# A gated cross-attention layer with a mixture of experts: expert weights loaded by another engine, in another order, and router steps moved between softmax sums

## The reference

```python
x = x + tanh(g_xattn[0]) * attn(ctx_768, layernorm(x), mask, ...)
xf = layernorm(x).reshape(-1, 256)
probs = softmax(xf @ w_router); topk_w, topk_idx = top_k(probs, 2)
h = gelu(einsum('te,ieh->tih', xf, w1) + b1)      # 8 experts
out = sum_over_experts((einsum('tih,ihe->tie', h, w2) + b2) * weights)
x = x + tanh(g_ffn[0]) * out
```

## Time and profile before

| | |
|---|---|
| median of 3 runs | 947.58 us (947.28 to 949.43) |
| the profiled execution | 946.13 us |
| its span | 944.6 us, TensorE's mean clock 0.975 |
| TensorE busy | 863.5 us (91%) |
| VectorE busy | 647.5 us (69%) |
| ScalarE busy | 514.6 us (54%) |
| GpSimd busy | 354.5 us (38%) |
| DMA | 70.3 MB, mean 74 GB/s |

### The profile page before, as it was taken

How to read it: one execution, slowest core, us unless ns; L and a number is a source line. 1 busy time by engine, 2 the same in 40 slices (tenths; PEclk the granted TensorE clock), 3 DMA queues, 4 the chain that set the end, 5 groups by cost and what they waited for, 6 DMA issues and landing times.

```text
span 944.6 us, 19200 instructions
## 1 busy us (share of the span) xinstructions
PE 863.5 (91%) x5968; PEld 662.2 (70%) x5968; DVE 647.5 (69%) x1500; ACT 514.6 (54%) x1371; POOL 354.5 (38%) x270
## 2 busy tenths in 40 slices
PE   3898899998999998999899998999999999999865
PEld 3654445554455444544369998999999999999855
DVE  6767766767867668665886787765757675765655
ACT  2668675787757877477652843433434343433432
POOL 2333223332375234652073247342422442242433
PEclk8899999999999999999999998999999999999977
DMA  4801000130012201120053368352432553252441
GB/s 123 237 1 48 1 1 1 45 92 1 12 51 74 90 23 35 57 79 1 1 182 67 80 175 230 62 139 45 124 55 45 133 128 55 45 139 45 123 114 20
DMA packets 58793, 70.30 MB, mean 74 GB/s; under 512 B 11536, under 2 KB 51856, under 8 KB 58736
## 3 DMA queue, kind: packets, MB, share of 16 engines
q0 software_dynamic: 17520, 32.49, 15.5%
q1 hardware_dynamic: 40224, 37.10, 13.7%
q10 hardware_dynamic: 992, 0.00, 0.1%
HBM read 44.04 MB, written 26.31 MB: 74 GB/s over the span
## 4 chain that ended last, share of the span: by engine, by line
PE 51%; issue 15%; DVE 12%; POOL 10%; ACT 5%; DMA 4%; DVEq 1%; POOLq 0%; SPq 0%; ACTq 0%
PE psS L1642 19%; PE psF L1838 9%; PE psO L1838 9%; POOL rr L635 6%; PE psO L1775 4%; PE psS L1759 4%; POOL routed L645 3%; DVE p_sum L1115 3%; PE psF L1642 2%; DMA b_raw<-in_L_ffn_b 2%; DMA lnf<-routed 2%; PE psF L1806 1%; ACT sq L807 1%; ACT p_ring L851 1%; DMA xr<-in_x 1%
## 5 line engine op out<-in xcount | busy, mean ns | idle before, releaser
L868 ACT ACTIVATE V<-psS,b_col 128x256 f32<-128x256 f32 x280 | 117.2, 471 | 222.8 <-PE psS L1642 209.3
L659 POOL DMA_INDIRECT out<-V,token_i x70 | 121.0, 1729 | 260.7 <-DVE V L1304 247.7
L635 POOL TENSOR_TENSOR rr<-ssm,minus_half 128x4 f32<-128x4 f32 (+1 forms) x72 | 119.9, 1666 | 255.5 <-DVE ssm L1079 255.4
L851 ACT ACTIVATE p_ring<-psS,shift 128x1024 f32<-128x1024 f32 x128 | 136.7, 1112 | 75.9 <-PE psS L1759 72.7
L1775 PE MATMUL psO<-p_ring,V 128*64 128x512 f32 x576 | 150.3, 619 | 4.6 <-ACT o_sb L839 4.6
L1115 DVE TENSOR_TENSOR p_sum<-p_sum,p_ring 128x1024 f32<-128x1024 f32 (+1 forms) x112 | 136.0, 1214 | 0.7
L1838 PE MATMUL psF<-ln_hi,K 128*128 128x256 f32 x560 | 123.0, 283 | 0.0
L1759 PE MATMUL psS<-Q,K 64*128 64x512 f32 x864 | 121.7, 413 | 0.1
L1759 PEld LDWEIGHTS psS<-Q,K 64*128 64x128 f32 x864 | 77.0, 187 | 61.8 <-issue 43.5
L1838 PE MATMUL psO<-ln_hi,K 128*128 128x256 f32 x560 | 120.0, 278 | 0.0
L1642 PE MATMUL psS<-w_hi 128*128 128x256 f32 x280 | 83.2, 297 | 20.1 <-DVE w_lo L1267 13.4
(11 more groups left out here) (294 smaller groups left out, 1804.3 us busy)
## 6 DMA issues: line engine op xcount, KB each, us to landing
lnf<-routed SPq DMA_DIRECT2D x35, 258.0 KB, 2.8
xr<-in_L_ffn_w POOLq DMA_DIRECT2D x7, 1024.0 KB, 7.2
xn<-in_L_ffn_w POOLq DMA_DIRECT2D x7, 1024.0 KB, 8.8
routed<-pad_rows SPq DMA_DIRECT2D x17, 258.0 KB, 8.6
xr<-in_x SPq DMA_DIRECT2D x8, 512.0 KB, 4.6
xb<-in_x SPq DMA_DIRECT2D x4, 1024.0 KB, 6.0
out<-xb SPq DMA_DIRECT2D x4, 1024.0 KB, 4.7
xr<-in_L_ffn_w SPq DMA_DIRECT2D x4, 1024.0 KB, 6.7
```

The source lines that it names most:

```text
L635: pool.tensor_tensor(rr[0:p, c % 2, n], ssm[0:p, c % 2, n], minus_half[0:p, n], ALU.pow).then_inc(rr_ready, 1)
L659: pool.indirect_dma_start(out_rows, bass.IndirectOffsetOnAxis(ap=token_i[:, m:m + 1], axis=0), y_out[:, m, :], None, bounds_check=NTOK - 1 ...
L851: act.activation(p_ring[0:p, u % RING, :], psS[u % 2][0:p].rearrange("p a n -> p (a n)"), ACT.Exp, bias=bias).then_inc(exp_done, 1)
L868: act.activation(g32[:, q % 2, (c % 2) * TM:(c % 2 + 1) * TM], psH[q][:, (c % 2) * TM:(c % 2 + 1) * TM], ACT.Gelu_apprx_tanh, bias=b1_col[ ...
```

## The change

1. SyncE issues the weight loads of all experts; GpSimd none. One count per buffer (`w1_loaded`, `w2_loaded`, `b1_loaded`) takes the place of one for four loads. Each engine waits for the part that it reads.
2. w1 is loaded once w1 is cut, w2 and b2 once w2 is cut (and b2 copied), apart from each other.
3. In SyncE's list these loads stand between loads of rows; in its loop tile t first loads the next w1 (if t is an expert's last tile), then rows of tile t+2, then w2, b2, b1.
4. On VectorE, in the last window, `add_probabilities` of a group goes ahead of its router steps, `router_rows` to its group's end, and the two cuts of w2 from groups 3 and 4 to 5 and 8.

The diff:

```diff
@@ -546,11 +548,30 @@
 
-    def load_weights(e):
+    def load_w1(e):
         sp.wait_ge(w1_ready, (e - 1) * 2 * KEPT + 2)
+        sp.dma_start(w1_raw, w1[e].rearrange("(c p) h -> p c h", p=P)).then_inc(w1_loaded, 16)
+
+    def load_w2(e):
         sp.wait_ge(w2_ready, (e - 1) * 2 * KEPT + 2)
         sp.wait_ge(w_cut, e)
+        sp.dma_start(w2_raw, w2[e].rearrange("(c p) d -> p c d", p=P)).then_inc(w2_loaded, 16)
+        sp.dma_start(b2_raw[:], b2[e:e + 1].to_broadcast([P, D])).then_inc(w2_loaded, 16)
+
+    def load_b1(e):
         sp.wait_ge(b1_taken, e)
-        sp.dma_start(w1_raw, w1[e].rearrange("(c p) h -> p c h", p=P)).then_inc(raw_loaded, 16)
-        sp.dma_start(w2_raw, w2[e].rearrange("(c p) d -> p c d", p=P)).then_inc(raw_loaded, 16)
-        sp.dma_start(b1_raw[:], b1[e].rearrange("(c p) -> p c", p=P)).then_inc(raw_loaded, 16)
-        sp.dma_start(b2_raw[:], b2[e:e + 1].to_broadcast([P, D])).then_inc(raw_loaded, 16)
+        sp.dma_start(b1_raw[:], b1[e].rearrange("(c p) -> p c", p=P)).then_inc(b1_loaded, 16)
+
+    def next_w1(t, turn, e):
+        sp.wait_ge(w1_ready, t * 2 + 4)
+        sp.sem_inc(passed, 1)
+        sp.dma_start(w1_raw, w1[bass.ds(e, 1)].rearrange("a (c p) h -> p (a c) h", p=P)).then_inc(w1_loaded, 16)
+
+    def next_w2(t, turn, e):
+        sp.wait_ge(w2_ready, t * 2 + 4)
+        sp.sem_inc(passed, 1)
+        sp.wait_ge(w_cut, turn + (KE + 1))
+        sp.wait_ge(b1_taken, turn + (KE + 1))
+        sp.sem_inc(passed, 1)
+        sp.dma_start(w2_raw, w2[bass.ds(e, 1)].rearrange("a (c p) d -> p (a c) d", p=P)).then_inc(w2_loaded, 16)
+        sp.dma_start(b2_raw[:], b2[bass.ds(e, 1)].to_broadcast([P, D])).then_inc(w2_loaded, 16)
+        sp.dma_start(b1_raw[:], b1[bass.ds(e, 1)].rearrange("a (c p) -> p (a c)", p=P)).then_inc(b1_loaded, 16)
 
@@ -564,3 +585,5 @@
     load_rows(1, kept_row(1))
-    load_weights(1)
+    load_w1(1)
+    load_w2(1)
+    load_b1(1)
     sp.wait_ge(scattered, (B - 1) * (32 * T))
@@ -570,5 +593,8 @@
     load_rows(4, kept_row(4))
+    load_w1(2)
+    load_w2(2)
     load_rows(5, kept_row(5))
-    load_weights(2)
+    load_b1(2)
     load_rows(6, kept_row(6))
+    load_w1(3)
     sp.wait_ge(pads_known, 1)
@@ -576,3 +602,5 @@
         pad(e)
+    load_w2(3)
     load_rows(7, kept_row(7))
+    load_b1(3)
     for e in range(NE // 2, NE):
@@ -580,3 +608,2 @@
     load_rows(8, kept_row(8))
-    load_weights(3)
     sp.wait_ge(scattered, B * (32 * T))
@@ -585,5 +612,21 @@
     load_rows(KTILES, sp.value_load(tile_row[0:1, KTILES:KTILES + 1], min_val=0, max_val=NE * REGION - TM))
+    load_w1(KE + 1)
+    load_rows(KTILES + 1, sp.value_load(tile_row[0:1, KTILES + 1:KTILES + 2], min_val=0, max_val=NE * REGION - TM))
+    load_w2(KE + 1)
+    load_b1(KE + 1)
     tiles = sp.value_load(tile_count[0:1, 0:1], min_val=SURE, max_val=NTILES)
-    with sp.Fori(KTILES, NTILES - 1) as t, sp.If(t + 1 < tiles):
-        load_rows(t + 1, sp.value_load(tile_row[0:1, bass.ds(t + 1, 1)], min_val=0, max_val=NE * REGION - TM))
+    with sp.Fori(KTILES, NTILES) as t, sp.If(t < tiles):
+        turn = sp.value_load(tile_switch[0:1, bass.ds(t, 1)], min_val=0, max_val=NE - 1)
+        after = sp.value_load(tile_next[0:1, bass.ds(t, 1)], min_val=0, max_val=NE - 1)
+        with sp.If(turn > 0):
+            with sp.If(turn < NE - 1):
+                next_w1(t, turn, after)
+            sp.sem_inc(passed, 1)
+        with sp.If(t + 2 < tiles):
+            load_rows(t + 2, sp.value_load(tile_row[0:1, bass.ds(t + 2, 1)], min_val=0, max_val=NE * REGION - TM))
+        with sp.If(turn > 0):
+            with sp.If(turn < NE - 1):
+                next_w2(t, turn, after)
+            sp.sem_inc(passed, 1)
+        sp.sem_inc(passed, 1)
     sp.wait_ge(x_loaded, tiles * 16)
@@ -648,8 +691,2 @@
 
-    def load_expert(e):
-        pool.dma_start(w1_raw, w1[bass.ds(e, 1)].rearrange("a (c p) h -> p (a c) h", p=P)).then_inc(expert_loaded, 16)
-        pool.dma_start(w2_raw, w2[bass.ds(e, 1)].rearrange("a (c p) d -> p (a c) d", p=P)).then_inc(expert_loaded, 16)
-        pool.dma_start(b1_raw[:], b1[bass.ds(e, 1)].rearrange("a (c p) -> p (a c)", p=P)).then_inc(expert_loaded, 16)
-        pool.dma_start(b2_raw[:], b2[bass.ds(e, 1)].to_broadcast([P, D])).then_inc(expert_loaded, 16)
-
     def add_rows(t):
@@ -661,16 +698,2 @@
 
-    def add_and_load(t):
-        turn = next_expert(pool, t)
-        add_rows(t)
-        with pool.If(turn > 0):
-            with pool.If(turn < NE - 1):
-                pool.wait_ge(w1_ready, t * 2 + 4)
-                pool.sem_inc(passed, 1)
-                pool.wait_ge(w2_ready, t * 2 + 4)
-                pool.sem_inc(passed, 1)
-                pool.wait_ge(w_cut, turn + (KE + 1))
-                pool.wait_ge(b1_taken, turn + (KE + 1))
-                pool.sem_inc(passed, 1)
-                load_expert(pool.value_load(tile_next[0:1, bass.ds(t, 1)], min_val=0, max_val=NE - 1))
-
     first_root(0)
@@ -712,12 +735,7 @@
     pool.wait_ge(x2_stored, 16 * B)
-    pool.wait_ge(w1_ready, 2 * KTILES + 2)
-    pool.wait_ge(w2_ready, 2 * KTILES + 2)
-    pool.wait_ge(w_cut, KE + 1)
-    pool.wait_ge(b1_taken, KE + 1)
-    load_expert(KE + 1)
     with pool.Fori(KTILES, SURE) as t:
-        add_and_load(t)
+        add_rows(t)
     tiles = count_of(pool)
     with pool.Fori(SURE, NTILES) as t, pool.If(t < tiles):
-        add_and_load(t)
+        add_rows(t)
 
@@ -870,3 +888,5 @@
 
-    def change_first(t):
+    def change_first(t, e):
+        act.wait_ge(w1_loaded, e * 16)
+        act.sem_inc(passed, 1)
         for part in w1_parts:
@@ -874,2 +894,3 @@
         act.wait_ge(gelu_done, t * HC + 2 * HC)
+        act.wait_ge(b1_loaded, e * 16)
         act.sem_inc(passed, 1)
@@ -879,2 +900,4 @@
         act.wait_ge(expert_done, t * MH + MH)
+        act.wait_ge(w2_loaded, e * 32)
+        act.sem_inc(passed, 1)
         for part in w2_parts:
@@ -887,4 +910,3 @@
         with act.If(turn > 0):
-            act.wait_ge(expert_loaded, turn * 64)
-            change_first(t)
+            change_first(t, turn + KE)
             change_second(t, turn + KE)
@@ -968,4 +990,3 @@
         if t % KEPT == KEPT - 1:
-            act.wait_ge(raw_loaded, 64 * (e + 1))
-            change_first(t)
+            change_first(t, e)
         if t == 2:
@@ -1273,2 +1294,4 @@
     def new_bias(e):
+        dve.wait_ge(w2_loaded, e * 32)
+        dve.sem_inc(passed, 1)
         dve.tensor_copy(b2_row[:], b2_raw[:]).then_inc(w_cut, 1)
@@ -1427,7 +1450,2 @@
             router_slots(b - 1)
-        if not even and past and last and i == 3:
-            router_softmax(b - 1)
-        if not even and past and last and i == 4:
-            router_largest(b - 1, 1)
-            router_rows(b - 1)
         if g >= 1:
@@ -1436,2 +1454,6 @@
             router_logits(b - 1)
+        if not even and past and last and i == 3:
+            router_softmax(b - 1)
+        if not even and past and last and i == 4:
+            router_largest(b - 1, 1)
         if turned_at(g) is not None:
@@ -1483,2 +1505,4 @@
             router_largest(b - 1, 0)
+        if not even and past and last and i == 4:
+            router_rows(b - 1)
         if not even and past and not last:
@@ -1494,4 +1518,4 @@
             dve.tensor_copy(b2_row[:], b2_raw[:]).then_inc(w_cut, 1)
-        if w + 1 == WINDOWS and i in (3, 4):
-            cut(w2_parts[i - 3:i - 2], i - 3, w2_ready)
+        if w + 1 == WINDOWS and i in (5, 8):
+            cut(w2_parts[i // 8:i // 8 + 1], i // 8, w2_ready)
         if w + 1 == WINDOWS and i in (6, 7):
```

More of the change, by code:

```diff
@@ L76, in flamingo_gated_layer @@
         tile_count = persistent.enter_context(nc.sbuf_tensor("tile_count", [P, 1], I32))
-        tile_row = persistent.enter_context(nc.sbuf_tensor("tile_row", [P, NTILES], I32))
+        tile_row = persistent.enter_context(nc.sbuf_tensor("tile_row", [P, NTILES + 2], I32))
         tile_switch = persistent.enter_context(nc.sbuf_tensor("tile_switch", [P, NTILES], I32))
@@ L313, in flamingo_gated_layer @@
             xT_ready = sem("xT_ready")
-            expert_loaded = sem("expert_loaded")
+            w1_loaded = sem("w1_loaded")
+            w2_loaded = sem("w2_loaded")
+            b1_loaded = sem("b1_loaded")
             cut_hi_ready = sem("cut_hi_ready")
@@ L1427, in _ @@
                         router_slots(b - 1)
+                    if g >= 1:
+                        add_probabilities(2 * g - 2)
+                    if not even and past and i == (2 if last else 3):
+                        router_logits(b - 1)
                     if not even and past and last and i == 3:
@@ L1431, in _ @@
                         router_largest(b - 1, 1)
-                        router_rows(b - 1)
-                    if g >= 1:
-                        add_probabilities(2 * g - 2)
-                    if not even and past and i == (2 if last else 3):
-                        router_logits(b - 1)
                     if turned_at(g) is not None:
```

## The result

The changed kernel takes **937.8 us** (median of 4 runs, 935.8 to 940.48) against 948.5 us for the kernel before (4 runs, 947.28 to 951.0): ratio 0.9892, 95% interval 0.9869 to 0.9916, 10.7 us less. I read each trace by its parts and leave the sum to the medians.

The account below looks back on a forecast made before the run. The prediction took TensorE to be the bound in the expert stage, with waits at three places. Terms of -17.5, -2.0, +4.4, +3.0 and -1.2 summed to -13.3 us, giving 934.3 us, range 928.5 to 942.

Parts of the forecast that it names:

- Term 4: Tile 7: its rows, issued later behind expert 3's weights and pads, land late; +4.4 us (0 to +7).
- Term 1: Last two expert switches: weights issued earlier by SyncE end TensorE's waits for w1's cut; -17.5 us.
- Term 3: Expert switches: rows queued behind w1 land 0.5 us late at six switches, +3.0; two short waits go, -1.2 us.
- Term 5: Last pair of heads: VectorE's new order shortens TensorE's wait for o_sb; -2.0 us (0 to -3.1).
- the early load is not early: Last switches: w1, asked for early, itself waits, so half of that gain stays away; 943 us, chance 0.08.
- Term 2: GpSimd: loses four DMA issues per switch and a table read, but nothing waits for its adds sooner; 0 us.
- Term 6: Static switches of experts 1 and 2, the loop's extra table reads and longer tile_row: 0 us.
- pair of heads gives nothing: Last pair of heads: same VectorE work, clock may drop in the new idle; 936.3 or 938.8 us, chance 0.15.
- rows come in time: Tile 7 and switches: rows 7 cost 2.0 us at most, the switches nothing; 928.9 us, chance 0.18.
- The slow rival: Switches and tile 7: rows wait for whole weight loads, 3.0 us late at six switches; 951.9 to 967 us, chance 0.05.

Follow-up runs that it names:

- e12: e10 with ScalarE also waiting for all four transfers of the expert before it cuts w1; 940.22 us.
- e10: e1 with the next w1 in SyncE's loop issued together with w2, behind both cuts, counts still separate; 929.11 us.
- e9: Kernel before with GpSimd still loading the weights, but w1 early, the rest behind the add, and separate counts; 932.17 us.
- e5: e1 with the rows of tile t + 2 issued ahead of the next expert's w1 in SyncE's loop; 925.42 us.
- e1: Changed kernel with SyncE's list reordered so that the rows of tile 7 go ahead of w1 and w2 of expert 3; 929.14 us.
- e14: e5 with w2's second cut moved behind the low part of tile 0's turn; 927.0 us.
- e4: e1 with w2's second cut moved behind the low part of tile 0's turn; 928.68 us.
- e3: Kernel before with only VectorE's new order in the last pair of heads and the moved cuts of w2; 945.80 us.
- e2: e1 with VectorE's order of before in the last pair of heads; 932.37 us.

## Why the prediction was right, and where not

Forecast 934.3 us, result 937.8, in the range of 928.5 to 942. The sign and the main term were right. That the gain came out near (13.3 us forecast, 10.7 measured) is partly luck. Term 4 was 4.7 us too small and the end of the kernel cost 1.3 us that I had at 0, 6.0 us in all; against it, terms 1, 3 and 5 left out 4.1 us of gain (0.6, 2.3 and 1.2). The range was also narrower than it says: it takes in "the bounds of terms 3 to 5", but the upper bound of term 3 (3.0 us at six switches, 18 instead of 3) leads to 949.3, outside of 942.

- **Term 1, the last two switches: right.** Forecast -17.5 us; 35.37 instead of 53.43 is -18.1. The reason was incomplete: I wrote of the early issue of w1. The runs put 8.2 to 10.5 us on the separate counts, 4.7 on SyncE as the issuing engine (e12), and 2.3 to 3.3 on the early w1 once the counts are separate. The rival "the early load is not early" would have cost little as far as it means a late issue: e10 does just that.
- **Term 2, GpSimd 0: right.** In e9 it keeps the work and nothing waits for its adds.
- **Term 3, rows behind w1: right in sign, too large.** Forecast +3.0; e5 against e1 gives 2.5 us for it, the columns of all kernels 1.7, e14 against e4 0.4. The -1.2 for the short waits that go is in the table too: 272.21 before and 271.68 in the changed kernel, with the new price already in it.
- **Term 4, rows of tile 7: the step that failed, mis-sized.** Forecast +4.4 (0 to +7); measured +11.4 in the trace from add 0 to add 8, and 8.7 to 9.1 us by e1. Two steps of it failed. Issue: "at about 574.1" was 576.13. SyncE's own issues grew long with much under way: w2's took 0.95 us and b2's 1.49, where the same two took 0.37 and 0.56 at 909.74 and 910.29 in the same trace. Landing: "I take 582" was 588.5, and the upper bound of 584.3 was passed too. The prediction doesn't derive that bound; it is what the 10.8 us of w2 give from an issue at 573.5, as if the rows came with w2. They were issued 2.6 us behind w2 and landed 12.4 us after their own issue, and w2 and b2 took until 587.4, 13.9 us from w2's issue, with pads and scatters beside them. The remainder of the working held: 9.1 us from landing to first layer (9.2 forecast), and 2.3 us back from the clock (5.99 instead of 8.24 us for 48 products; 2.5 forecast).
- **Term 5, last pair of heads: right, on the low side.** Forecast -2.0 (0 to -3.1); e3 and e2 both give 3.2, a little past the bound.
- **Term 6, others 0: one miss.** From add 34 to the end of the span takes 7.9 us in all eleven kernels with SyncE's loop and 6.5 to 6.6 in the three without (before, e3, e9): +1.3 us at the very end that I had not looked for. It lies in SyncE's last step, from 936.31 to 938.47 us in the changed kernel and from 943.73 to 944.49 before. Its cause wasn't tried.

The rival "pair of heads gives nothing" is refuted by e2 and e3, though the profiled execution looked just like it. The rival "rows come in time" is refuted by the 14.7 us. The slow rival had the right place and the wrong size: rows behind w1 are late by tenths of a us, not 3.0.

Summed by measured parts: -18.1 - 3.2 + 9.1 (e1) + 1.3 - 0.5 = -11.4, against -10.7 by the medians.
